# Early zero transfers on GpSimd's queue, and node counts summed by VectorE before TensorE

## The chip, the cores and the metric

The kernel runs on one core of a Trainium2 chip. The metric is the device time of one execution in microseconds. TensorE (PE) multiplies matrices, VectorE (DVE) and ScalarE (ACT) do elementwise work, GpSimd (POOL) does elementwise work and issues transfers, and SyncE (SP) only issues transfers. SP and POOL each have a transfer queue of their own, as ACT has.

## The reference

A two-layer graph network on 625 nodes with 1024 features. What the change touches is in the first layer: an edge list with eight edge types is turned into counts, for every type a table of how many edges run from each node to each node, and the messages are means over them.

```python
def _rgcn(x, edge_index, edge_type, weight, root, bias):
    src, dst = (edge_index[0], edge_index[1])
    msgs = x[src]
    out = x @ root + bias
    n = x.shape[0]
    for r in range(weight.shape[0]):
        mask = (edge_type == r).astype(x.dtype)
        sums = jax.ops.segment_sum(msgs * mask[:, None], dst, num_segments=n)
        cnt = jax.ops.segment_sum(mask, dst, num_segments=n)
        mean = sums / jnp.maximum(cnt, 1.0)[:, None]
        out = out + mean @ weight[r]
    return out
```

A gate, a linear attention and two feed-forward blocks stand around it; the second layer uses the counts of all types again.

## The kernel before

Weights stream from memory in chunks of 128 x 512: SP loads a chunk into one of four staging buffers, an engine splits it into a high part (`w_hi`) and a low part (`w_lo`), and TensorE multiplies with both (`three`, lines 363 to 365). A load waits until the chunk four places ahead of it is split. A group is eight chunks; its results, five tiles of 125 rows, go from PSUM to a ring in SBUF and from there, by POOL's queue, to memory (`pre`). Groups 0 to 9 run first.

**Scatter stage, beside groups 3 to 5.** VectorE works out a position for every edge (ranks, tables, `packed_buckets`, which gives the mark `mk_ranked`). Then 15 scatter steps follow, each with 11 columns of edges. In a step VectorE writes two one-hot tiles for each column (`sc_hi`, `sc_lo`, lines 912 and 913), ScalarE scales one (`sc_code`, line 918), TensorE multiplies them (line 923) between the dense matmuls, and one weight chunk is split: its high part on ScalarE after the third column, its low part on VectorE after the fifth. Step s splits chunk 36 + s. After step 8 VectorE evacuates group 4 (line 479); for that the ring's tiles must have been stored.

The counts are gathered in `adj`, a tile of 125 partitions and 40 x 626 16-bit integers, in the SBUF that the rank tables occupied. It must be zeroed after the tables and before the first counts are added (at 231.9 us). 19 transfers from a tile of zeros do that, each 125 rows by 2636 bytes, on SP's queue: eight in a row after the load of chunk 39, then one after each of the next 11 loads (line 1051). The tile of zeros is written by ScalarE after the evacuation of group 2 (line 1045).

**Relation loop, from about 375 us.** For each of eight edge types VectorE turns the five count tiles (five times 125 source nodes) into a high and a low half-precision part (`a_hi`, `a_lo`). TensorE multiplies ones by them and accumulates all five tiles, which gives the number of edges into each node (`counts_pe`, line 1353: five matmuls for each of two column halves; the low parts are skipped by a branch unless a count is large). VectorE turns that into a reciprocal (`rcnt`). TensorE aggregates node features by counts (line 1406, 160 matmuls a round), VectorE multiplies by the reciprocal (`mtmp`, line 1556), ScalarE copies the high part (line 1456) and VectorE subtracts for the low part (line 1548). Two dense groups follow, with one head pair of an attention between their matmuls (lines 1371 to 1392, VectorE's front of it at lines 1506 to 1513). The counts of the next round are multiplied between the two dense groups.

Each engine runs its own program in order, and the waits between them are on semaphores. These lines give the order on SP:

```python
            if c == LAST_AHEAD:
                wait(SP, mk_zeros)
                wait(SP, mk_ranked)
                for i in range(EARLY):
                    zero_counts(i)
            if c > LAST_AHEAD:
                zero_counts(EARLY + c - LAST_AHEAD - 1)
```

Of the kernel before, what the change touches and what calls it, by code (L numbers as in the profile page):

```python
# [18 lines left out]
P, T = 125, 5  # L19
# [34 lines left out]
def build(nc, a, out):  # L54
# [226 lines left out]
    for g in range(G_PRE0):  # L281
        for m in range(T):
            POOL.wait_ge(S("bank_free"), (g + 1) * T + m + 1)
            if g in TURNED0:
                b, c = PIECES[m]
                POOL.dma_start(pre_t0[L0_ORDER[g] - 4, b][:, c], ring_t[:, b, c]).then_inc(S(f"stpre0_{m}"), 16)
            else:
                POOL.dma_start(pre[L0_ORDER[g], m], ring[:, m, :]).then_inc(S(f"stpre0_{m}"), 16)  # L288

    POOL.wait_ge(S("split_done"), NST + C_BACK)  # L290
    POOL.wait_ge(S("rcnt"), 1)
    for c in range(C_BACK, C_BACK + (-C_BACK) % NSL):
        split_chunk(c, c % NSL, c // NST + 1)
    split_rounds(C_BACK + (-C_BACK) % NSL, C_PROJ + KT)
    POOL.wait_ge(S("feed_full"), KT)
    for g in range(2):
        POOL.dma_start(z[:, :, g * 512:(g + 1) * 512], pre[2 + g].rearrange("t p f -> p t f")).then_inc(S("ld_z"), 16)
    for c in range(C_PROJ + KT, C_L1):
        split_low(c, c % NSL)
    POOL.wait_ge(S("split_done"), NST + C_L1 + NSL)  # L300
    split_rounds(C_L1 + NSL, nloop * NSL)
    for c in range(nloop * NSL, NSTREAM):
        split_chunk(c, c % NSL, c // NST + 1)
# [401 lines left out]
    ZERO, ZERO_RUN = NBUCKET * NB // 2 + 1, 659  # L705
    assert ZERO % ZERO_RUN == 0
# [299 lines left out]
    def beside(dense, evacuate_plain, evacuate, evacuate_half, load_bias):  # L1006
# [38 lines left out]
        mk_zeros = sig(ALE.activation(zeros[:], zero[0:P, :].to_broadcast([P, ZERO_RUN]), ACT.Copy), "act_step")  # L1045

# [6 lines left out]
        EARLY = ZERO // ZERO_RUN - 11  # L1053
        for c in range(SC0 * KT, (SC0 + SC_GROUPS) * KT):
            load_chunk(c, c % NSL, (L0_ORDER[c // KT] - c // KT) * KT)
            if c == LAST_AHEAD:
                wait(SP, mk_zeros)
                wait(SP, mk_ranked)
                for i in range(EARLY):
                    zero_counts(i)  # L1060
            if c > LAST_AHEAD:
                zero_counts(EARLY + c - LAST_AHEAD - 1)
        for g in TURNED0:
            for s in range(KT):
                load_block(g * KT + s, s, L0_ORDER[g] * KT, s)
                if g == TURNED0[0] and s < 3:
                    zero_counts(EARLY + 8 + s)
# [46 lines left out]
        DVE.wait_ge(S("ld_bt"), 16 + 16 * (ZERO // ZERO_RUN))  # L1114
# [49 lines left out]
        ALE.wait_ge(S("ld_bt"), 16 + 16 * (ZERO // ZERO_RUN))  # L1164
# [143 lines left out]

    counts_split(0)
# [35 lines left out]
    def counts_pe(r):  # L1345

        PE.wait_ge(S("a_hi"), r + 1)
        for i in range(2):
            bank, h0, hn = ag_bank(i)
            PE.wait_ge(S("ag_free"), r * 18 + i + 1)  # L1350

            def add(a16, t, first, last):
                return PE.matmul(ps[:, bank, 0:hn], ones16[0:P, :], a16[:, t, h0:h0 + hn], start=first, stop=last)

            for t in range(T - 1):
                add(a_hi, t, t == 0, False)
            with PE.If(many):
                PE.wait_ge(S("a_ready"), r + 1)
                for t in range(T):
                    add(a_lo, t, False, False)  # L1360
            add(a_hi, T - 1, False, True).then_inc(S("ag_full"), 1)

# [33 lines left out]
    def relation_pe(r, more):  # L1396
# [45 lines left out]
    counts_pe(0)  # L1442
# [98 lines left out]
    def relation_dve(r, more):  # L1541
# [9 lines left out]
        for j in range(16):  # L1551
# [6 lines left out]

            DVE.wait_ge(S("ag_free"), 3 + r * 18 + i + 1)
            DVE.sem_inc(S("ag_scaled"), 1)  # L1560
# [7 lines left out]
        if more:  # L1568
            counts_split(r + 1)
            DVE.wait_ge(S("a_ready"), r + 2)  # L1570
# [1043 lines left out]
    def evac_turned(g, b):  # L2614

        if (g, b) == (1, 0):
            DVE.wait_ge(S("ld_bt"), 32 + 16 * (ZERO // ZERO_RUN))
# [474 lines left out]
```

## Time and profile before

| what | value |
|---|---|
| median of 3 runs | 1828.2 us (1827.75 to 1829.06) |
| the profiled execution's own time | 1828.82 us |
| its span in the profile | 1827.3 us |
| TensorE busy | 1738.4 us, 95% of the span |
| VectorE busy | 989.4 us, 54% |
| ScalarE busy | 461.8 us, 25% |
| GpSimd busy | 712.6 us, 39% |
| mean granted TensorE clock | 0.979 of full speed |

The span is the time from the first to the last instruction in the profile; 1.5 us of the time lie around it. Busy time is of instructions that compute; issuing a transfer is not in it. TensorE's matmuls overlap, so a busy TensorE may still have room, and only a stretch in which it waits, or the chain of work that ended last, tells what sets the end.

### The profile page before, as it was taken

The page shows a single profiled execution, that of the slowest core. Times are in us where ns is not written, and L with a number is a line of the kernel's source. Part 1 is how long each engine was busy: PE and PEld are TensorE (multiplying, and loading weights), DVE is VectorE, ACT ScalarE, POOL GpSimd, SP SyncE. Part 2 cuts the span into 40 slices and gives each one's busy share as a digit, 9 for nine tenths or more (in the row PEclk, how much of TensorE's full clock was granted, in tenths as well). Part 3 has the DMA queues.
Part 4 walks back from the last instruction along what each step waited for, and adds up shares of the span by engine and source line. Part 5 has one row for each costly group of instructions (what it writes and reads, how often), then busy time and mean ns, then how long its engine had stood idle before and what let it go on. Part 6 is the DMA issues. An engine that isn't in the chain of part 4 may idle for free.

```text
span 1827.3 us, 27442 instructions
## 1 busy us (share of the span) xinstructions
PE 1738.4 (95%) x9548; PEld 1438.4 (79%) x9548; DVE 989.4 (54%) x2498; ACT 461.8 (25%) x888; POOL 712.6 (39%) x613
## 2 busy tenths in 40 slices
PE   6998999999999999999999999846999999999999
PEld 4775699978777777878787877634999888879987
DVE  6997999972625454452526386877613234352311
ACT  3327788930101011010101154433000000111100
POOL 3100010036363544536453544000785551446862
PEclk9999999999999999999999999858999999999999
DMA  4435333243131212122233532110454350113322
GB/s 132 142 115 163 124 109 94 94 129 94 47 97 38 87 40 80 52 68 69 63 89 122 168 113 86 28 48 7 131 183 142 103 155 25 47 47 126 91 72 67
DMA packets 132122, 168.42 MB, mean 92 GB/s; under 512 B 14383, under 2 KB 75963, under 8 KB 131767
## 3 DMA queue, kind: packets, MB, share of 16 engines
q1 hardware_dynamic: 104213, 128.21, 23.6%
q10 hardware_dynamic: 21730, 22.51, 3.8%
q0 software_dynamic: 6080, 16.40, 2.9%
q8 instruction: 60, 0.98, 0.2%
q14 instruction: 39, 0.32, 0.1%
HBM read 135.51 MB, written 25.30 MB: 88 GB/s over the span
## 4 chain that ended last, share of the span: by engine, by line
PE 81%; DVE 10%; DMA 3%; ACT 2%; DVEq 2%; issue 2%; POOL 1%; SPq 1%; ACTq 0%
PE ps L363 21%; PE ps L364 21%; PE ps L365 21%; PE ps L1406 9%; DMA w_stage<-in_stream 2%; PE ps L1001 1%; DVE w_lo L314 1%; PE ps L1371 1%; PE ps L923 1%; DVE key_start L869 1%; POOL w_lo L272 1%; PE ps L1326 1%; SPq L1051 1%; DMA nat<-in_x 1%; DVE scan L784 1%
## 5 line engine op out<-in xcount | busy, mean ns | idle before, releaser
L363 PE MATMUL ps<-w_hi,xt_hi 128*125 128x512 f32 x1320 | 539.4, 409 | 12.1 <-DVE xt_lo L552 3.5
L252 POOL TENSOR_TENSOR w_hi<-w_stage,zero 128x512 fp32r<-128x512 f32 x258 | 278.1, 1078 | 680.0 <-PE ps L365 650.8
L364 PE MATMUL ps<-w_lo,xt_hi 128*125 128x512 f32 x1320 | 523.6, 397 | 0.0
L365 PE MATMUL ps<-w_hi,xt_lo 128*125 128x512 f32 x1320 | 522.0, 395 | 0.0
L255 POOL TENSOR_TENSOR w_lo<-w_stage,w_hi 128x512 fp32r<-128x512 f32 x258 | 351.2, 1361 | 20.2
L363 PEld LDWEIGHTS ps<-w_hi,xt_hi 128*125 128x125 f32 x1320 | 247.0, 187 | 70.9 <-DVE xt_lo L552 4.3
L365 PEld LDWEIGHTS ps<-w_hi,xt_lo 128*125 128x125 f32 x1320 | 246.4, 187 | 63.3
L364 PEld LDWEIGHTS ps<-w_lo,xt_hi 128*125 128x125 f32 x1320 | 246.6, 187 | 53.4
L363 PE MATMUL ps<-xt_hi,w_hi 128*128 128x314 f32 x736 | 240.9, 327 | 0.8 <-DVE ring L2612 0.7
L365 PE MATMUL ps<-xt_hi,w_lo 128*128 128x314 f32 x736 | 226.0, 307 | 0.0
L364 PE MATMUL ps<-xt_lo,w_hi 128*128 128x314 f32 x736 | 225.8, 307 | 0.0
L363 PEld LDWEIGHTS ps<-xt_hi,w_hi 128*128 128x128 f32 x736 | 138.9, 189 | 1.8 <-POOL w_lo L255 1.1
L364 PEld LDWEIGHTS ps<-xt_lo,w_hi 128*128 128x128 f32 x736 | 139.5, 190 | 0.3
L365 PEld LDWEIGHTS ps<-xt_hi,w_lo 128*128 128x128 f32 x736 | 139.0, 189 | 0.0
L1590 DVE TENSOR_TENSOR nat<-nat,ps 125x512 f32<-125x512 f32 x80 | 53.0, 686 | 121.6 <-PE ps L365 121.3
L1456 ACT ACTIVATE xt_hi<-mtmp 128x313 fp32r<-128x313 f32 (+1 forms) x128 | 59.5, 465 | 196.1 <-DVEq L1560 196.1
L1406 PE MATMUL ps<-a_hi,xn_hi 125*128 125x313 f16 (+1 forms) x640 | 106.4, 297 | 2.0 <-DVE mtmp L1556 1.9
L1406 PE MATMUL ps<-a_hi,xn_lo 125*128 125x313 f16 (+1 forms) x640 | 106.3, 296 | 0.0
L309 ACT ACTIVATE w_hi<-w_stage 128x512 fp32r<-128x512 f32 x116 | 71.8, 628 | 102.7 <-PE ps L365 53.7
L971 ACT ACTIVATE counts<-ps 125x628 int16<-125x628 f32 x120 | 82.0, 691 | 20.9 <-PE ps L1001 19.6
L288 POOL DMA_DIRECT2D pre<-ring x30 | 15.9, 534 | 180.0 <-ACT ring L462 98.0
L1406 PEld LDWEIGHTS ps<-a_hi,xn_hi 125*128 125x128 f16 x640 | 61.4, 97 | 27.5 <-DVE mtmp L1556 3.4
(433 smaller groups left out, 2178.5 us busy)
## 6 DMA issues: line engine op xcount, KB each, us to landing
w_stage<-in_stream SPq DMA_DIRECT2D x374, 256.0 KB, 2.7
pre<-ring POOLq DMA_DIRECT2D x30, 250.0 KB, 5.6
adj<-zeros SPq DMA_DIRECT2D x19, 321.8 KB
a_qt<-pre_t SPq DMA_DIRECT2D x18, 312.5 KB, 3.8
a_qt<-pre_t ACTq DMA_DIRECT2D x14, 312.5 KB
pre_t<-ring_t POOLq DMA_DIRECT2D x12, 312.5 KB, 3.1
pre_t<-ring_t ACTq DMA_DIRECT2D x12, 312.5 KB
a_vx<-pre SPq DMA_DIRECT2D x9, 312.5 KB
```

The lines of the kernel that those rows point to most:

```text
L252: POOL.tensor_tensor(w_hi[:, q, :], w_stage[:, q % NST, :], zero[:].to_broadcast([128, 512]), ALU.add).then_inc(S("hi_done"), 1)
L255: POOL.tensor_tensor(w_lo[:, q, :], w_stage[:, q % NST, :], w_hi[:, q, :].bitcast(F32), ALU.subtract).then_inc(S("split_done"), 1)
L272: POOL.tensor_tensor(w_lo[:, q, :], w_stage[:, q % NST, :], w_hi[:, q, :].bitcast(F32), ALU.subtract).then_inc(S("split_done"), 1)
L309: ALE.activation(w_hi[:, c % NSL, :], w_stage[:, c % NST, :], ACT.Copy).then_inc(S("hi_done"), 1)
L314: DVE.tensor_tensor(w_lo[:, c % NSL, :], w_stage[:, c % NST, :], w_hi[:, c % NSL, :].bitcast(F32), ALU.subtract).then_inc(S("split_done"), 1)
L363: PE.matmul(dst, l_hi, r_hi, start=first, stop=False)
L364: PE.matmul(dst, l_hi, r_lo, start=False, stop=False)
L365: return PE.matmul(dst, l_lo, r_hi, start=False, stop=last)
L971: ALE.activation(counts[g % 4][:], ps[0:P, b:b + 2, 0:SPLIT], ACT.Copy).then_inc(S("hi_main"), 1)
L1406: return PE.matmul(dst, x16[:, t, k * 128:(k + 1) * 128], a16[:, t, h0:h0 + hn], start=first, stop=last)
L1456: ALE.activation(xt_hi[:, j // 2, h0:h0 + hn], mtmp[j % 4][:, 0:hn], ACT.Copy).then_inc(S("mt_hi"), 1)
L1590: DVE.tensor_tensor(u_, u_, ps[0:P, m, :], ALU.add).then_inc(S("bank_free"), 1)
```

## The change

The eight early zero transfers go to POOL's queue, ahead of its stores of group 3, with a semaphore of their own; SP keeps the other eleven. ScalarE writes the tile of zeros before the evacuation of group 0. In rounds 2 to 8 VectorE sums the five count tiles as 16-bit integers, splits the one sum into a high and a low half-precision part, and TensorE multiplies ones by these two, for two column halves: four matmuls for ten and no branch. Round 1 keeps the old form. In the aggregation VectorE no longer waits for its own multiply to signal ScalarE; ScalarE waits for the semaphore of the multiply itself.

```diff
+    def gpsimd_program(mk_zeros, mk_ranked, zero_counts):
+
+        for g in range(G_PRE0):
+            if g == 3:
+                wait(POOL, mk_zeros)
+                wait(POOL, mk_ranked)
+                for i in range(EARLY):
+                    zero_counts(POOL, i, "ld_zero")
+            for m in range(T):
+                POOL.wait_ge(S("bank_free"), (g + 1) * T + m + 1)
...
+        mk_zeros = sig(ALE.activation(zeros[:], zero[0:P, :].to_broadcast([P, ZERO_RUN]), ACT.Copy), "act_step")
         for g in range(3):
             ahead = (g + 2) * KT - (2 if g == 0 else 1)
...
-        mk_zeros = sig(ALE.activation(zeros[:], zero[0:P, :].to_broadcast([P, ZERO_RUN]), ACT.Copy), "act_step")
...
-        def zero_counts(i):
-            SP.dma_start(adj[:].bitcast(F32)[:, i * ZERO_RUN:(i + 1) * ZERO_RUN], zeros[:]).then_inc(S("ld_bt"), 16)
...
+        def zero_counts(eng, i, landed):
+            eng.dma_start(adj[:].bitcast(F32)[:, i * ZERO_RUN:(i + 1) * ZERO_RUN], zeros[:]).then_inc(S(landed), 16)
...
             if c == LAST_AHEAD:
                 wait(SP, mk_zeros)
                 wait(SP, mk_ranked)
-                for i in range(EARLY):
-                    zero_counts(i)
             if c > LAST_AHEAD:
-                zero_counts(EARLY + c - LAST_AHEAD - 1)
+                zero_counts(SP, EARLY + c - LAST_AHEAD - 1, "ld_bt")
...
+    def counts_sum(r):
+
+        t_ = adj[:, bass.ds(r * T * NB, T * NB)].rearrange("p (t x) -> p t x", x=NB)
+        DVE.tensor_tensor(tile_pairs[:], t_[:, 0:2], t_[:, 2:4], ALU.add)
+        DVE.drain()
+        DVE.tensor_tensor(tile_sum[:], tile_pairs[:, 0], tile_pairs[:, 1], ALU.add)
+        DVE.drain()
+        DVE.tensor_tensor(tile_sum[:], tile_sum[:], t_[:, 4], ALU.add)
+        DVE.drain()
+        DVE.tensor_copy(sum_hi[:], tile_sum[:])
+        DVE.drain()
+        DVE.tensor_tensor(sum_lo[:], tile_sum[:], sum_hi[:], ALU.subtract).then_inc(S("a_ready"), 1)
...
+    def sums_pe(r):
+
+        PE.wait_ge(S("a_ready"), 2 * r + 1)
         for i in range(2):
             bank, h0, hn = ag_bank(i)
             PE.wait_ge(S("ag_free"), r * 18 + i + 1)
...
+            dst = ps[:, bank, 0:hn]
+            PE.matmul(dst, ones16[0:P, :], sum_hi[:, h0:h0 + hn], start=True, stop=False)
+            PE.matmul(dst, ones16[0:P, :], sum_lo[:, h0:h0 + hn], start=False, stop=True).then_inc(S("ag_full"), 1)
...
-            counts_pe(r + 1)
+            sums_pe(r + 1)
...
-            ALE.wait_ge(S("ag_scaled"), r * 16 + j + 1)
+            ALE.wait_ge(S("ag_free"), r * 18 + j + 6)
...
-
-            DVE.wait_ge(S("ag_free"), 3 + r * 18 + i + 1)
-            DVE.sem_inc(S("ag_scaled"), 1)
...
             counts_split(r + 1)
-            DVE.wait_ge(S("a_ready"), r + 2)
+            counts_sum(r + 1)
+            DVE.wait_ge(S("a_ready"), 2 * r + 3)
```

The order of instructions at the places that matter. On SP, at the end of the loop over the first loads and after it, before the change:

```order
L198 REGISTER_ALU
L198 COMPARE_AND_BRANCH
L185 DMA w_stage<-in_stream 128x512 [waits split_done] x8
L1051 DMA adj<-zeros 125x659 [waits dve_step,act_step]
L1051 DMA adj<-zeros 125x659 x7
L185 DMA w_stage<-in_stream 128x512 [waits split_done]
L1051 DMA adj<-zeros 125x659
```

And with it:

```order
L198 REGISTER_ALU
L198 COMPARE_AND_BRANCH
L185 DMA w_stage<-in_stream 128x512 [waits split_done] x8
L185 DMA w_stage<-in_stream 128x512 [waits split_done,dve_step,act_step]
L1058 DMA adj<-zeros 125x659
```

The load of chunk 40, which stood behind eight zero transfers, now follows the loads of chunks 32 to 39 directly, and one zero transfer follows it. On POOL, from its first loads to the stores of the groups (`pre`, five a group; `pre_t` are groups in turned layout), before the change:

```order
L212 DMA nat<-in_x 125x1024 [waits ld_x2]
L212 DMA nat<-in_x 125x1024
L272 TENSOR_TENSOR w_lo<-w_stage,w_hi 128x512 [waits hi_done] x8
L288 DMA pre<-ring 125x512 [waits bank_free] x30
L286 DMA pre_t<-ring_t 128x625 [waits bank_free] x3
```

And with it:

```order
L212 DMA nat<-in_x 125x1024 [waits ld_x2]
L212 DMA nat<-in_x 125x1024
L272 TENSOR_TENSOR w_lo<-w_stage,w_hi 128x512 [waits hi_done] x8
L295 DMA pre<-ring 125x512 [waits bank_free] x15
L1058 DMA adj<-zeros 125x659 [waits dve_step,act_step]
L1058 DMA adj<-zeros 125x659 x7
L295 DMA pre<-ring 125x512 [waits bank_free] x15
```

The eight zero transfers stand between the stores of group 2 and those of group 3. On VectorE, in the body of the relation loop after the last low part of the aggregation, before the change:

```order
L1304 COPY a_hi<-adj 125x3130
L1305 REGISTER_ALU
L1306 TENSOR_TENSOR a_lo<-adj,a_hi 125x3130
L1572 ISA
L1572 TENSOR_TENSOR adj<-adj 125x3130
L1506 TENSOR_REDUCE a_mx<-ps 125x8 x2
```

And with it:

```order
L1311 COPY a_hi<-adj 125x3130
L1312 REGISTER_ALU
L1313 TENSOR_TENSOR a_lo<-adj,a_hi 125x3130
L1324 ISA
L1324 TENSOR_TENSOR tile_pairs<-adj 125x1252
L1326 TENSOR_TENSOR tile_sum<-tile_pairs 125x626
L1328 ISA
L1328 TENSOR_TENSOR tile_sum<-tile_sum,adj 125x626
L1330 CAST sum_hi<-tile_sum 125x626
L1332 TENSOR_TENSOR sum_lo<-tile_sum,sum_hi 125x626
L1603 REGISTER_ALU
L1605 ISA
```

Five computing instructions stand between the split of the counts and the addition that carries the counts of all types along (line 1572 before, 1605 now), behind which the attention's front follows.

## Rows read from the trace of the kernel before

**Rows 1.** Page, part 1: busy us, share of the span and instructions of each engine.

```profile
PE 1738.4 (95%) x9548; PEld 1438.4 (79%) x9548; DVE 989.4 (54%) x2498; ACT 461.8 (25%) x888; POOL 712.6 (39%) x613
```

**Rows 2.** Windows: us, busy us of each engine, TensorE clock, DMA share, GB/s.

```profile
160.00:170.00 10.00, 4.97 (x19) 2.78 (x18) 4.12 (x22) 4.00 (x11) 0.00 (x0) 0.76 0.50 168
```

**Rows 3.** Chain that ended last, around 142 us: start us, us, what.

```profile
142.14 23.30 DMA w_stage<-in_stream
```

**Rows 4.** Timeline of SP: start us, us, instruction, count.

```profile
129.80 12.30 SPq L1051 DMA_DIRECT2D adj<-zeros  x8
142.14 2.89 SPq L185 DMA_DIRECT2D w_stage<-in_stream  x1
```

**Rows 5.** Timeline of ScalarE, scatter steps 2 to 4 (brackets: idle before, releaser).

```profile
150.13 0.61 ACT L309 ACTIVATE w_hi<-w_stage 128x512 fp32r<-128x512 f32 x1
...
155.01 0.61 ACT L309 ACTIVATE w_hi<-w_stage 128x512 fp32r<-128x512 f32 x1
...
165.47 0.63 ACT L309 ACTIVATE w_hi<-w_stage 128x512 fp32r<-128x512 f32 x1 [5.49 <-DMA w_stage<-in_stream]
```

**Rows 6.** Timeline of VectorE, scatter steps 0, 4 and 8.

```profile
138.07 0.69 DVE L314 TENSOR_TENSOR w_lo<-w_stage,w_hi 128x512 fp32r<-128x512 f32 x1 [0.28 <-ACT w_hi L309]
...
166.13 0.69 DVE L314 TENSOR_TENSOR w_lo<-w_stage,w_hi 128x512 fp32r<-128x512 f32 x1 [5.88 <-ACT w_hi L309]
...
188.35 3.27 DVE L479 TENSOR_TENSOR ring<-ps,bias_pre 125x512 f32<-125x512 f32 x5
```

**Rows 7.** Timeline of TensorE, scatter steps 4 and 8.

```profile
160.22 0.48 PE L923 MATMUL ps<-sc_hi,sc_code 125*128 125x240 bf16 x3
...
166.44 0.67 PE L923 MATMUL ps<-sc_hi,sc_code 125*128 125x240 bf16 x2 [5.03 <-ACT sc_code L918]
...
186.92 0.48 PE L923 MATMUL ps<-sc_hi,sc_code 125*128 125x240 bf16 x3
```

**Rows 8.** Chain that ended last, relation loop: counts, aggregation of two rounds.

```profile
431.03 1.35 PE ps L1353 x10
...
544.93 21.35 PE ps L1406 x160
...
628.46 21.35 PE ps L1406 x160
```

**Rows 9.** Transfers, 131 to 141 us: GB/s in 40 slices; packets, MB, engines' share.

```profile
GB/s 107 197 229 246 229 188 148 139 130 117 145 116 137 127 127 127 105 127 137 116 137 127 127 137 116 137 127 116 137 127 137 116 127 137 127 127 127 137 116 127
...
q1 hardware_dynamic: 612, 1.39, 36.6%
```

**Rows 10.** Transfers, 16 to 25 us: GpSimd's queue (packets, MB, share); its loads.

```profile
q0 software_dynamic: 288, 1.02, 46.0%
...
nat<-in_x POOLq DMA_DIRECT2D x2, 500.0 KB, 6.2
```

**Rows 11.** Timeline of VectorE, the last table of ranks.

```profile
126.33 0.40 DVE L906 SCALAR_TENSOR_TENSOR g_start<-g_bucket,g_half 1x240 int32<-1x240 f32 x1
```

**Rows 12.** Timeline of GpSimd, 110 to 146 us, and its stores' time to landing.

```profile
113.39 0.53 POOL L288 DMA_DIRECT2D pre<-ring  x1 [0.17 <-issue]
142.11 2.64 POOL L288 DMA_DIRECT2D pre<-ring  x5 [28.18 <-ACT ring L462]
...
DMA to landing us min/median/max: 2.7/5.6/15.0
```

**Rows 13.** Timeline of ScalarE, between groups 0 and 1.

```profile
54.26 1.28 ACT L309 ACTIVATE w_hi<-w_stage 128x512 fp32r<-128x512 f32 x2 [7.00 <-DMA w_stage<-in_stream]
```

**Rows 14.** Timeline of VectorE in one round, before the attention's front.

```profile
570.81 2.38 DVE L1572 TENSOR_TENSOR adj<-adj  x1 [0.17 <-DVE a_lo L1306]
579.02 1.29 DVE L1506 TENSOR_REDUCE a_mx<-ps 125x8 f32<-125x512 f32 x2 [5.83 <-PE ps L1371]
```

**Rows 15.** Instructions on `adj`: ns min/median/max, first and last start, forms.

```profile
L1304 DVE CAST a_hi<-adj x8: 970/972/976, 372.7 to 901.9; 125x3130 f16 x7, 125x3130 f16<-125x3130 int16 x1
...
L1596 DVE TENSOR_REDUCE va<-adj x1: 3408/3408/3408, 985.4 to 985.4; 125x5 f32<-125x3130 int16 x1
```

**Rows 16.** Timeline of the first round's aggregation.

```profile
379.51 2.10 DVE L1500 RECIPROCAL rcnt<-rcnt 128x312 f32<-128x312 f32 x1
...
382.36 0.84 PE L1406 MATMUL ps<-a_hi,xn_hi 125*128 125x313 f16 x5 [1.43 <-DVE mtmp L1556]
```

More of the change, by code:

```diff
@@ L279, in build @@
     PIECES = [(0, slice(0, NODES)), (1, slice(0, NODES)), (2, slice(0, NODES)), (3, slice(0, 314)), (3, slice(314, NODES))]
[L281 to L300, printed above, removed]
@@ L301, in build @@
-    split_rounds(C_L1 + NSL, nloop * NSL)
-    for c in range(nloop * NSL, NSTREAM):
-        split_chunk(c, c % NSL, c // NST + 1)
+    def gpsimd_program(mk_zeros, mk_ranked, zero_counts):
[7 more added lines that the diff above has]
+                POOL.wait_ge(S("bank_free"), (g + 1) * T + m + 1)
+                if g in TURNED0:
+                    b, c = PIECES[m]
+                    POOL.dma_start(pre_t0[L0_ORDER[g] - 4, b][:, c], ring_t[:, b, c]).then_inc(S(f"stpre0_{m}"), 16)
+                else:
+                    POOL.dma_start(pre[L0_ORDER[g], m], ring[:, m, :]).then_inc(S(f"stpre0_{m}"), 16)
+        POOL.wait_ge(S("split_done"), NST + C_BACK)
+        POOL.wait_ge(S("rcnt"), 1)
+        for c in range(C_BACK, C_BACK + (-C_BACK) % NSL):
+            split_chunk(c, c % NSL, c // NST + 1)
+        split_rounds(C_BACK + (-C_BACK) % NSL, C_PROJ + KT)
+        POOL.wait_ge(S("feed_full"), KT)
+        for g in range(2):
+            POOL.dma_start(z[:, :, g * 512:(g + 1) * 512], pre[2 + g].rearrange("t p f -> p t f")).then_inc(S("ld_z"), 16)
+        for c in range(C_PROJ + KT, C_L1):
+            split_low(c, c % NSL)
+        POOL.wait_ge(S("split_done"), NST + C_L1 + NSL)
+        split_rounds(C_L1 + NSL, nloop * NSL)
+        for c in range(nloop * NSL, NSTREAM):
+            split_chunk(c, c % NSL, c // NST + 1)
@@ L705, in build @@
     ZERO, ZERO_RUN = NBUCKET * NB // 2 + 1, 659
+    EARLY = ZERO // ZERO_RUN - 11
     assert ZERO % ZERO_RUN == 0
@@ L1066, in beside @@
                 if g == TURNED0[0] and s < 3:
-                    zero_counts(EARLY + 8 + s)
+                    zero_counts(SP, EARLY + 8 + s, "ld_bt")
         for c in range(C_REL, C_REL + AHEAD):
@@ L1113, in beside @@
             split_dve(chunk_beside(s))
-        DVE.wait_ge(S("ld_bt"), 16 + 16 * (ZERO // ZERO_RUN))
+        DVE.wait_ge(S("ld_bt"), 16 + 16 * (ZERO // ZERO_RUN - EARLY))
+        DVE.wait_ge(S("ld_zero"), 16 * EARLY)
         DVE.wait_ge(S("sc_pe"), sc_per + EC + 1)
@@ L1163, in beside @@
             dense(h + HI0, hist_step(h))
-        ALE.wait_ge(S("ld_bt"), 16 + 16 * (ZERO // ZERO_RUN))
+        ALE.wait_ge(S("ld_bt"), 16 + 16 * (ZERO // ZERO_RUN - EARLY))
+        ALE.wait_ge(S("ld_zero"), 16 * EARLY)
         wait(ALE, mk_slots)
@@ L1307, in counts_split @@
                           ALU.subtract).then_inc(S("a_ready"), 1)
+    tile_pairs = at("tile_pairs", [P, 2, NB], I16, R_EXTRA)
+    tile_sum = at("tile_sum", [P, NB], I16, R_EXTRA + 2560)
+    sum_hi = at("sum_hi", [P, NB], F16, R_EXTRA)
+    sum_lo = at("sum_lo", [P, NB], F16, R_EXTRA + 1280)
+    def counts_sum(r):
[9 more added lines that the diff above has]
+        DVE.tensor_tensor(sum_lo[:], tile_sum[:], sum_hi[:], ALU.subtract).then_inc(S("a_ready"), 1)
     counts_split(0)
@@ L1343, in ag_bank, with counts_pe @@
         return 5 + i % 3, *halves[i % 2]
-    def counts_pe(r):
-        PE.wait_ge(S("a_hi"), r + 1)
+    def counts_pe():
+        PE.wait_ge(S("a_hi"), 1)
         for i in range(2):
             bank, h0, hn = ag_bank(i)
-            PE.wait_ge(S("ag_free"), r * 18 + i + 1)
+            PE.wait_ge(S("ag_free"), i + 1)
             def add(a16, t, first, last):
@@ L1357, in counts_pe @@
             with PE.If(many):
-                PE.wait_ge(S("a_ready"), r + 1)
+                PE.wait_ge(S("a_ready"), 1)
                 for t in range(T):
@@ L1361, in counts_pe @@
             add(a_hi, T - 1, False, True).then_inc(S("ag_full"), 1)
+    def sums_pe(r):
+        PE.wait_ge(S("a_ready"), 2 * r + 1)
+        for i in range(2):
+            bank, h0, hn = ag_bank(i)
+            PE.wait_ge(S("ag_free"), r * 18 + i + 1)
+            dst = ps[:, bank, 0:hn]
+            PE.matmul(dst, ones16[0:P, :], sum_hi[:, h0:h0 + hn], start=True, stop=False)
+            PE.matmul(dst, ones16[0:P, :], sum_lo[:, h0:h0 + hn], start=False, stop=True).then_inc(S("ag_full"), 1)
     def att_pe_b(r):
@@ L2616, in evac_turned @@
         if (g, b) == (1, 0):
-            DVE.wait_ge(S("ld_bt"), 32 + 16 * (ZERO // ZERO_RUN))
+            DVE.wait_ge(S("ld_bt"), 32 + 16 * (ZERO // ZERO_RUN - EARLY))
         if g - 1 not in TURNED1:
```

4 lines of the change are left out of this document (2 added, 2 removed).

## Prediction

> **What bounds the kernel now.** I read the page first, then the stretches in which TensorE waits, then the rows of the two places that the change touches. TensorE is busy 95% of the span [rows 1], so only two kinds of edit can move the end: one that takes away a TensorE stall, and one that takes matmuls out of a stretch where TensorE never waits. The change tries both.
>
> The stall lies in the scatter stage. In 160 to 170 us TensorE is busy 4.97 of 10 us, VectorE 4.12 and ScalarE 4.00, at a mean clock of 0.76 [rows 2]: all three wait together. The chain of waits names the cause, a weight chunk that took 23.30 us from issue to landing [rows 3]. SP's timeline shows why: it issues eight zero transfers in one run of 12.30 us, and only then, at 142.14, chunk 40 [rows 4]. ScalarE splits one chunk in each scatter step, 4.88 us apart (150.13, 155.01); the next split, of chunk 40, comes at 165.47 after 5.49 us of waiting for that load [rows 5]. VectorE, next in line, waits 5.88 us for ScalarE [rows 6], and TensorE 5.03 us [rows 7].
>
> The second place is the loop over relations. One round's 160 aggregation matmuls run as an unbroken piece of the chain, and so do the ten count matmuls between the two dense groups, 1.35 us [rows 8]: TensorE waits for nothing there, so what is cut from it comes off the end.
>
> **Eight zeros go from SP's queue to GpSimd's.** Their price on SP's queue: with zeros almost alone in flight the transfer engines are a third busy and move about 130 GB/s, so 8 x 321.8 KB (2.64 MB) need some 20 us, and chunk 40 stands behind them in the same queue [rows 9]. Loads of the same 125 rows on GpSimd's queue do better: two of them, 1.02 MB, took 46.0% of the time of 16 engines in a window of 9 us, beside SP's own transfers [rows 10], where SP's zeros with the queue almost to themselves get 36.6% [rows 9]. That is 66 us of engine time, so 2.64 MB need 171, or 10.7 us if all 16 share it; by the zeros' own 36.6% of 10 us for 1.39 MB [rows 9] it is 7.0. I expect the eight to land in about 10 us. They can start when the rank tables are done, after VectorE's last row of them at 126.33 + 0.40 [rows 11]. GpSimd is free then: its last store of group 2 is issued at 113.39 and its next, of group 3, only at 142.11; at about 0.7 us from issue to issue the eight take some 6 us [rows 12]. Nothing else waits behind them on GpSimd, and the stores of group 3 find their queue empty even if the zeros ran at SP's 130 GB/s to about 148 and pushed them back by 6 us, since VectorE asks for them only in its evacuation of group 4 (188.35 before, 182.8 after the shift below) [rows 6].
>
> The Trainium skill ("DMA: Bandwidth & Descriptors", section on why a DMA increments its semaphore by 16) says that a hardware queue uses the largest number of engines up to 16 that divides the rows, and GpSimd's queue can use 16 for a direct copy. 125 rows would give 5 of 16, or 31%; the trace's third and its 46.0% agree.
>
> Chunk 40 may be issued when chunk 36 is split, at 138.07 + 0.69 = 138.8 [rows 6], and SP is now free to do it. It has until 159.9 to land, 21 us; the loads between SP's other eleven zeros stay as they are. The 5.49 us wait then goes. The next limit is the step itself: 165.47 - (155.01 + 4.88) = **5.58 us**. VectorE carries this on, as it sets the 4.88 us pace and evacuates group 4. TensorE's own lag was larger: its first scatter matmuls of step 8 come at 186.92, and four steps after those of 160.22 they would come at 179.74, 7.2 us earlier [rows 7]; part of that is the low clock after its stall. VectorE does not gain that surplus, so 7.2 is the upper bound; 4.9 the lower, if a load lands 0.7 us late somewhere.
>
> **The zero tile is written earlier.** One ScalarE instruction moves from about 127.7 to about 41 us. There ScalarE soon waits 7.00 us for a load [rows 13], which hides its 0.7 us. Cost nothing; without that cover 0.7.
>
> **Count matmuls.** Seven of the eight rounds run ten matmuls before and four after: 6/10 of 1.35 = 0.81 us a round, **5.67 us**. The two skipped branches a round go too; I give them nothing. Bounds: 3.2 us, if a gap like the 2.5 us of issue idle over nine times (0.28 each) comes to show at each join and eats as much again (7 x 0.46); 6.5, if the slow first matmul behind them shortens too.
>
> VectorE pays for it with five instructions between the relation's last split and the attention's front. 16-bit adds of 3130 columns take 2.38 us [rows 14], 0.76 ns a column. So the pair sum (1252 columns) is about 1.0 us, two sums of 626 0.55 each, the copy 0.27 (0.972 us for 3130 [rows 15]), the difference 0.45, with drains about 3.2 us. From both sides: 1.6 us if all run as fast as the copy, 4.9 us as slow as the 16-bit reduction (3.408 us for 3130 [rows 15]). Behind them stands the attention's front, which today idles 5.83 us for TensorE's projection [rows 14]. Even 4.9 fits. Without that cover up to 4.9 us a round would fall on ScalarE's exponential, and then on TensorE's transposes.
>
> **The semaphore between multiply and copy goes.** VectorE no longer waits for its own multiply in order to signal ScalarE. In rounds 2 to 8 TensorE waits for neither. In the first round it does: 1.43 us at 382.36, behind a reciprocal that starts at 379.51, 0.15 us after the multiply before it ended [rows 16]. Two such gaps: **0.3 us**; bounds 0 and 1.0.
>
> **Sum.** 5.58 + 5.67 + 0.3 = 11.55 us. The profiled execution took 1828.82, so 1817.3 for it; it lies 0.6 above the median of the runs, so against the median of 1828.2 I say **1816.7 us**, with 1813.5 to 1820.1 from the bounds (8.1 to 14.7).
>
> **Rivals.**
>
> *Half the zeros' gain.* The transfers still run on the same engines, and only SP's time at issuing is saved. Then chunk 40 lands as long after its issue as before, but is issued 3.3 us earlier (138.8 for 142.14): 1828.2 - 3.3 - 5.67 - 0.3 = 1818.9. The third-busy row speaks against it: the delay is order within one queue, not full engines. Chance 0.08. The Trainium skill states this rule in the same page, section "Issuing engines are not separate DMA queues": issuing from several engines saves only the sequencer's time.
>
> *No gain from the zeros*, because another load is late in its place, say one of those after SP's remaining zeros: 1822.2. Those have 18 us and more to land. Chance 0.05.
>
> *No gain from the counts*, if four short matmuls with three waits show as long as ten did: 1822.4. Chance 0.05.
>
> *Slower: GpSimd's queue holds up the stores of group 3.* They stand behind the zeros in its order: 8 x 321.8 + 5 x 250.0 KB, 3.92 MB, must land between 126.7 and 182.8, or VectorE stops in its evacuation, with the scatter columns and splits queued behind it. That takes 70 GB/s; at 55 the stores land at 198, 15.2 us late, and the kernel is 0.2% slower than before. At 50 GB/s it would be 22.3 us: 1839.0. For it speaks a landing of 15.0 us for one of these stores [rows 12], against it that five of them needed only about 17 us then (75 GB/s) beside SP's zeros. Chance 0.04.
>
> *The change does nothing in sum*, both gains given back: 1828, chance 0.04.
>
> **How the numbers follow.** The forecast has 0.74. 0.2% (3.7 us) is about what a measurement can tell from no change. Faster by more: 0.74 + 0.08 + 0.05 + 0.05 = 0.92; same 0.04; slower 0.04. The range of 8 in 10 takes in the first rival and the forecast's bounds: 1813 to 1821.
>
> **What would show it.** ScalarE's splits of chunks 36 to 43 stand 4.9 us apart with no wait for a load but one at most, and the 0.76 clock is gone. Chunk 40 lands under 10 us after its issue. GpSimd's zero transfers keep the engines well above a third. A round of the relation loop falls from 83.5 (544.93 to 628.46 [rows 8]) to 82.7 us. VectorE's idle before the attention's front falls to about 2.6 us. I am wrong if a load or a store takes the wait over in 140 to 200, or if TensorE shows gaps around the four matmuls.

## The result and the profile after

The changed kernel takes 1817.44 us (median of 4 runs, 1816.58 to 1818.49) where the one before took 1828.63 beside it (4 runs, 1827.75 to 1829.64): ratio 0.9942, 95% interval 0.9926 to 0.9957, 11.2 us faster. The forecast was 1816.7 in a range of 1813 to 1821. The profiled execution took 1818.19 us, its span 1816.8 where that of before was 1827.3.

The page's first part [rows 1]: TensorE lost 42 matmuls (seven rounds, six fewer in each) and 6.5 us of busy time; VectorE gained 34 us of it, which no term of the sum had.

```profile
PE 1731.9 (95%) x9506; PEld 1434.6 (79%) x9506; DVE 1023.1 (56%) x2533; ACT 461.8 (25%) x888; POOL 717.8 (40%) x621
```

**The scatter stage.** The windows of the changed kernel, columns as in [rows 2]:

```profile
130.00:140.00 10.00, 10.00 (x48) 7.57 (x47) 9.46 (x24) 2.27 (x7) 2.31 (x5) 1.00 1.00 261
...
160.00:170.00 10.00, 10.00 (x57) 6.34 (x55) 9.44 (x49) 8.94 (x26) 0.00 (x0) 1.00 0.41 134
```

TensorE's hole in 160 to 170 is gone, with it the 0.76 of its clock. In 130 to 140 the transfer engines are busy all the time and move 261 GB/s, where for most of 131 to 141 they moved about 130 before [rows 9]. The list of transfers from 126 to 143 us says by which queue, and how long a transfer took to land:

```profile
q0 software_dynamic: 591, 2.46, 59.0%
q1 hardware_dynamic: 585, 1.07, 24.1%
...
adj<-zeros POOLq DMA_DIRECT2D x8, 321.8 KB, 9.6
```

GpSimd's queue alone has 59.0% of the engines' time, and a zero transfer lands 9.6 us after its issue. The view of the line that issues them adds the last start and the longest landing:

```profile
L1058 POOL DMA_DIRECT2D adj<-zeros x8: 530/530/533, 128.1 to 131.8; - x8
...
DMA to landing us min/median/max: 4.0/9.6/13.3
```

So the last of the eight has landed by 145.1 (131.8 + 13.3). SP's timeline, in place of the run of eight zeros [rows 4], and ScalarE's splits of chunks 39 to 41 [rows 5]:

```profile
128.35 11.62 SPq L185 DMA_DIRECT2D w_stage<-in_stream  x5
140.02 0.85 SPq L1058 DMA_DIRECT2D adj<-zeros  x1
```

```profile
155.79 0.61 ACT L316 ACTIVATE w_hi<-w_stage 128x512 fp32r<-128x512 f32 x1
160.67 0.61 ACT L316 ACTIVATE w_hi<-w_stage 128x512 fp32r<-128x512 f32 x1
165.54 0.62 ACT L316 ACTIVATE w_hi<-w_stage 128x512 fp32r<-128x512 f32 x1
```

Chunk 40 is the last of the five loads, issued by 139.97 and landed 6.1 us after its issue. Its split follows that of chunk 39 after 4.88 us and without a wait, where it took 10.46 before: 5.58 us less, to the hundredth.

Two waits of TensorE's are left between 140 and 215 us. One, of 1.94 us at 145.62, stood there before too (1.80 at 144.83). The other comes at VectorE's evacuation of group 4 and has grown, from 0.65 us before to 1.92; behind it the granted clock of 190 to 200 falls to a mean of 0.85, between its two levels of 1.2 and 2.4 GHz, where it was 1.00 before. The evacuation itself starts without a wait; its line stands first here, then TensorE's:

```profile
183.55 3.08 DVE L486 TENSOR_TENSOR ring<-ps,bias_pre 125x512 f32<-125x512 f32 x5
...
187.47 0.99 PE L931 MATMUL ps<-sc_hi,sc_code 125*128 125x240 bf16 x3 [1.92 <-ACT sc_code L926]
```

**The relation loop.** The chain of the changed kernel, at the count matmuls of the first round and at the aggregation of the two rounds that stand in [rows 8]:

```profile
425.43 0.15 PE ps L1395
425.58 0.13 PE ps L1396
425.71 0.13 PE ps L1395
425.84 0.13 PE ps L1396
...
537.73 21.35 PE ps L1441 x160
...
620.46 21.35 PE ps L1441 x160
```

Four matmuls run in 0.54 us with no gap where ten took 1.35, and a round takes 82.73 us instead of 83.53. The sums cost VectorE more than forecast. Its timeline in the round of [rows 14], and GpSimd's in the same microseconds:

```profile
563.25 1.65 DVE L1324 TENSOR_TENSOR tile_pairs<-adj 125x1252 int16 x1
564.98 1.42 DVE L1326 TENSOR_TENSOR tile_sum<-tile_pairs 125x626 int16<-125x626 int16 x1
566.57 1.07 DVE L1328 TENSOR_TENSOR tile_sum<-tile_sum,adj 125x626 int16<-125x626 int16 x1 [0.17 <-issue]
567.72 1.26 DVE L1330 CAST sum_hi<-tile_sum 125x626 f16<-125x626 int16 x1
569.05 0.49 DVE L1332 TENSOR_TENSOR sum_lo<-tile_sum,sum_hi 125x626 f16<-125x626 int16 x1
569.70 2.66 DVE L1605 TENSOR_TENSOR adj<-adj  x1 [0.16 <-DVE sum_lo L1332]
572.28 1.27 DVE L1541 TENSOR_REDUCE a_mx<-ps 125x8 f32<-125x512 f32 x2
```

```profile
562.66 1.57 POOL L252 TENSOR_TENSOR w_hi<-w_stage,zero 128x512 fp32r<-128x512 f32 x1 [22.46 <-PE ps L372]
564.31 1.75 POOL L255 TENSOR_TENSOR w_lo<-w_stage,w_hi 128x512 fp32r<-128x512 f32 x1
566.20 1.09 POOL L252 TENSOR_TENSOR w_hi<-w_stage,zero 128x512 fp32r<-128x512 f32 x1
567.38 1.42 POOL L255 TENSOR_TENSOR w_lo<-w_stage,w_hi 128x512 fp32r<-128x512 f32 x1
```

The five take 6.3 us (563.25 to 569.54), not 3.2, and VectorE no longer idles before the attention's front (L1541). Measured from the start of the round's aggregation the front comes 0.46 us later than before (34.55 us against 34.09). TensorE waits for none of it.

### The profile page after: what moved, and what is told of

Its sections match the earlier page's. It is cut to its first block, busy times and chain, and to the rows that moved or that the text cites. A ratio compares the mean times of both kernels' runs of the same rounds, so it can differ in the third digit from the quotient of the medians.

```text
span 1816.8 us, 27294 instructions
## 1 busy us (share of the span) xinstructions
PE 1731.9 (95%) x9506; PEld 1434.6 (79%) x9506; DVE 1023.1 (56%) x2533; ACT 461.8 (25%) x888; POOL 717.8 (40%) x621
## 4 chain that ended last, share of the span: by engine, by line
PE 80%; DVE 11%; ACT 3%; DMA 2%; DVEq 2%; issue 2%; POOL 0%; ACTq 0%; SPq 0%
PE ps L370 21%; PE ps L371 21%; PE ps L372 21%; PE ps L1441 9%; PE ps L1009 2%; ACT sc_code L926 1%; DVE w_lo L321 1%; DMA z<-pre 1%; PE ps L1406 1%; DVE key_start L877 1%; PE ps L1351 1%; DMA nat<-in_x 1%; DVE scan L792 1%; PE ps L1416 0%; PE ps L2509 0%
## 5 line engine op out<-in xcount | busy, mean ns | idle before, releaser
L1591 DVE TENSOR_TENSOR mtmp<-ps,rcnt 128x313 f32<-128x313 f32 (+1 forms) x128 | 61.7, 482 | 45.4 <-PE ps L1441 44.3
```

The lines of the kernel that those rows point to most:

```text
L1591: DVE.tensor_tensor(mtmp[j % 4][:, 0:hn], ps[:, bank, 0:hn], rcnt[:, h0:h0 + hn], ALU.mult).then_inc(S("ag_free"), 1)
```

## Experiments

All runs stand in one table: the time, its ratio to the kernel before measured beside it, and three marks of each trace. Stretch A runs from ScalarE's split of chunk 39 to the first relation's cast of its counts (`a_hi`), B from there to the last relation's cast, C from there to the end of the span. Six of the seven changed count blocks lie in B, the seventh in C. The kernel before took 1828.63 us beside the changed kernel, 1829.24 beside zeros_only, counts_only, semaphore_back and zeros_spread, 1829.63 beside zeros_act, sums_twice, sums_alone and two_matmuls, and 1829.26 beside the last two.

| kernel | median us | ratio, interval | chunk 39 | first cast | last cast | span | A | B | C |
|---|---|---|---|---|---|---|---|---|---|
| before | 1828.63 | | 155.01 | 372.72 | 901.95 | 1827.3 | 217.71 | 529.23 | 925.4 |
| changed | 1817.44 | 0.9942, 0.9926-0.9957 | 155.79 | 368.17 | 891.44 | 1816.8 | 212.38 | 523.27 | 925.4 |
| zeros_only | 1823.18 | 0.9966, 0.9954-0.9978 | 155.58 | 367.77 | 896.93 | 1820.2 | 212.19 | 529.16 | 923.3 |
| counts_only | 1822.39 | 0.9961, 0.9947-0.9975 | 156.09 | 373.86 | 897.22 | 1821.6 | 217.77 | 523.36 | 924.4 |
| semaphore_back | 1817.23 | 0.9943, 0.9930-0.9957 | 156.81 | 368.69 | 892.97 | 1815.2 | 211.88 | 524.28 | 922.2 |
| zeros_spread | 1820.34 | 0.9959, 0.9946-0.9973 | 155.10 | 369.95 | 893.24 | 1816.2 | 214.85 | 523.29 | 923.0 |
| zeros_act | 1819.15 | 0.9948, 0.9935-0.9962 | 154.75 | 368.79 | 892.03 | 1817.1 | 214.04 | 523.24 | 925.1 |
| sums_twice | 1817.64 | 0.9934, 0.9920-0.9948 | 155.17 | 367.55 | 890.84 | 1816.3 | 212.38 | 523.29 | 925.5 |
| sums_alone | 1820.65 (one run) | | 155.33 | 367.54 | 894.16 | 1819.3 | 212.21 | 526.62 | 925.1 |
| two_matmuls | 1815.53 | 0.9924, 0.9910-0.9937 | 156.23 | 368.59 | 890.16 | 1814.4 | 212.36 | 521.57 | 924.2 |
| low_part_branch | 1814.57 | 0.9923, 0.9909-0.9936 | 154.86 | 367.19 | 888.81 | 1813.1 | 212.33 | 521.62 | 924.3 |
| changed_again | 1817.95 | 0.9934, 0.9920-0.9948 | 154.88 | 367.25 | 890.55 | 1816.6 | 212.37 | 523.30 | 926.1 |

The intervals are 0.12 to 0.16% wide to either side, 2.2 to 2.8 us: they tell each part from the kernel before, but not one part from the other, nor single microseconds. A and B repeat far better: B is 523.24 to 523.36 us in the six traces with the changed kernel's relation loop (sums_twice, which changes only VectorE's part of it, among them).

### Each part alone

zeros_only is the kernel before with the zeros' part of the diff, counts_only the one with the rest:

```diff
# zeros_only
+                for i in range(EARLY):
+                    zero_counts(POOL, i, "ld_z")
# counts_only
-            counts_pe(r + 1)
+            sums_pe(r + 1)
...
-            ALE.wait_ge(S("ag_scaled"), r * 16 + j + 1)
+            ALE.wait_ge(S("ag_free"), r * 18 + j + 6)
```

> Only the eight zero transfers move to GpSimd's queue; count matmuls and the semaphore stay as before (the zeros count on a semaphore that is free until later). My theory (chunk 40 no longer stands behind the zeros, the step pace of 4.88 us is the next limit): the split of chunk 40 comes 4.88 us after that of chunk 39, the end of the scatter stage moves by 5.58 us, the kernel is 5.6 us faster (ratio 0.9969), 5.0 at the least if the wait at the evacuation of group 4 grows. Rival, that the zeros gave only SP's issue time: 3.3 us (0.9982). Rival, that what the trace of the whole change shows at 370 us (4.5 us) is all that is left of it at the end: 4.5 us (0.9975).

> Only the count matmuls and the semaphore change; the zeros stay on SP's queue and the 5.49 us wait for chunk 40 stays. My theory after the trace of the whole change: 7 x 0.80 us of matmuls and 1.06 us in the first round, 6.7 us faster (ratio 0.9963); the period of a round is 82.7 us. By the terms of the prediction (0.3 us for the semaphore): 6.0 us (0.9967). Rival, that the join costs as much as the matmuls saved: about 1 us or less. If the two parts add up, this and the kernel with the zeros alone give 11 to 12 us together.

Measured: 6.1 us (1829.24 - 1823.18) and 6.9 us (1829.24 - 1822.39). In the traces zeros_only shortens A by 5.52 us and leaves B (0.07), counts_only shortens B by 5.87 and leaves A (0.06). By the stretches the parts add up (5.52 + 5.87 against 5.33 + 5.96 in the changed kernel), and each has its own place. By the medians they give 13.0 us against 11.2, which the intervals allow but which shows no sum. The rivals with half the zeros' gain or none, and with none from the counts, fall: 3.3 us, and also 4.5, lie below A's 5.5.

### The semaphore put back

```diff
-            ALE.wait_ge(S("ag_free"), r * 18 + j + 6)
+            ALE.wait_ge(S("ag_scaled"), r * 16 + j + 1)
...
+            DVE.wait_ge(S("ag_free"), 3 + r * 18 + i + 1)
+            DVE.sem_inc(S("ag_scaled"), 1)
```

The zeros are counted on the semaphore `ld_z` here, as in zeros_only; the rest is the changed kernel.

> The changed kernel with the semaphore between multiply and copy put back: VectorE waits for its own multiply and then signals ScalarE, as before. If the 1.06 us that the first round gained beyond the matmuls is the semaphore's: TensorE's waits for the mean at the start of the first round come back (about 1.4, 0.45 and 0.5 us in place of less), the aggregation of round 2 starts 1.0 us later, measured from the end of the histogram stage, and the rounds from the second on keep 82.7 us; the kernel is 1 us slower than the changed one, about 10 us faster than before (ratio 0.9944). If it is 0.3 us as predicted: round 2 starts 0.3 us later. Rival, that the later rounds also hang on it: their period grows beyond 82.8 us.

Against the changed kernel's 523.27, B is 1.01 us longer. From the first cast to the aggregation of round 2 it is 0.91 of that, and the later rounds keep 82.73 us, so the rival with a longer period falls. TensorE's waits from 360 to 400 us, of this kernel and of the changed one (in total, times, longest):

```profile
PE ps L1441 <- DVE mtmp L1591: 1.9, 2, 1.4
```

```profile
PE ps L1441 <- DVE mtmp L1591: 1.2, 1, 1.2
```

0.7 us of the 1.0 are these waits, all in the first round. VectorE runs behind TensorE there (in the changed kernel until 388 us, here past 391), so each multiply's wait for itself (0.23 us between `mtmp` and the next instruction) adds up over many multiplies, not over two. The total time, 1817.23, is not the 1 us above the changed kernel that was expected: its C is 3.1 us shorter, in stages of which the edit touches only the last round's multiplies.

### Order in the queue, or engines to carry it

Two other ways to take the eight zeros out from in front of chunk 40, both on a hardware queue: behind the loads on SP's own queue, and on ScalarE's.

```diff
# zeros_spread: on SP, behind each load from chunk 40 on
                 zero_counts(SP, EARLY + c - LAST_AHEAD - 1, "ld_bt")
+                zero_counts(SP, c - LAST_AHEAD - 1, "ld_zero")
# zeros_act: on ScalarE, behind each of its first eight splits
+                    if s < EARLY:
+                        if s == 0:
+                            wait(ALE, mk_ranked)
+                        zero_counts(ALE, s, "ld_zero")
```

> The changed kernel, but the eight zeros go back to SP's queue, one more behind each of the eight loads from chunk 40 on, so that chunk 40 itself stands in front of them. If the gain came from the order in one queue alone, and the rate in it is enough: 4.88 us from split to split, the same time as the changed kernel (0 to 0.5 us from it). If the rate of one hardware queue with 125 rows limits it (two zeros of 321.8 KB at 130 GB/s need 4.95 us, a load more, in a step of 4.88): each load lands later than the one before, by 1 to 2 us a step, and the wait for a load comes back after some six steps, with 3 to 10 us; the kernel is then 3 to 10 us slower than the changed one.

> The changed kernel, but the eight zeros are issued by ScalarE on its own queue, one behind each of its splits from 130 us on, in place of GpSimd's queue. If a queue of its own is what counts: 4.88 us from split to split to the end of the stage and the time of the changed kernel (within 1 us). If the few transfer engines that a hardware queue uses for 125 rows count, as with the zeros spread over SP's queue: SP's own zeros and ScalarE's need the same engines, loads land later and later, and a wait of 2 to 3 us comes back at the end of the stage, near 200 us, as it did there. If ScalarE is held up while it issues (SP's issues took 1.5 us each when its queue was full): steps of more than 4.88 us, up to 8 us in sum.

In both the split of chunk 40 follows after 4.9 us, without a wait; in zeros_spread

```profile
155.10 0.62 ACT L313 ACTIVATE w_hi<-w_stage 128x512 fp32r<-128x512 f32 x1
159.98 0.62 ACT L313 ACTIVATE w_hi<-w_stage 128x512 fp32r<-128x512 f32 x1
```

and in zeros_act from 154.75 to 159.62. The order was the cause of the stall of before. But a smaller wait comes back later. In zeros_spread ScalarE's splits near 200 us read

```profile
197.81 0.63 ACT L313 ACTIVATE w_hi<-w_stage 128x512 fp32r<-128x512 f32 x1 [0.62 <-DMA w_stage<-in_stream]
...
204.96 0.63 ACT L313 ACTIVATE w_hi<-w_stage 128x512 fp32r<-128x512 f32 x1 [2.16 <-DMA w_stage<-in_stream]
```

and in zeros_act

```profile
198.84 0.63 ACT L313 ACTIVATE w_hi<-w_stage 128x512 fp32r<-128x512 f32 x1 [2.04 <-DMA w_stage<-in_stream]
```

A is 2.47 and 1.66 us longer than in the changed kernel. From 126 to 215 us the loads' median time from issue to landing says why; the rows are of the changed kernel, zeros_spread and zeros_act:

```profile
w_stage<-in_stream SPq DMA_DIRECT2D x19, 256.0 KB, 4.3
```

```profile
w_stage<-in_stream SPq DMA_DIRECT2D x18, 256.0 KB, 11.7
```

```profile
w_stage<-in_stream SPq DMA_DIRECT2D x19, 256.0 KB, 10.1
```

A hardware queue of its own (ScalarE's) helps little: the loads land almost as late as with all zeros on SP's. Getting out of the order gives 5.58 us at chunk 40. What GpSimd's queue adds is that the eight are through by 145.1 us, ahead of most of the loads; with this A is 1.7 to 2.5 us shorter than in the two others, where a wait comes back near 200. These two runs change the time of issue with the queue: ScalarE issues its eight one a step, from 137.16 to 174.01, and GpSimd all of them from 128.1 to 131.8. So they don't show whether the early issue or the wider queue is worth the 1.7 to 2.5 us; no run issues the eight early, in one block, on a hardware queue other than SP's. The expectation by rate had the right kind and place, though for SP's queue a larger price (3 to 10 us). ScalarE was not held up: its first issue takes 1.35 us and the others 0.72 to 0.76, and they hide in its idle time. In total zeros_spread lies 2.9 us above the changed kernel's 1817.44 and zeros_act 1.7, differences that the intervals don't part.

### What VectorE's sums cost, and how much is hidden

```diff
# sums_twice
+            counts_sum(r + 1, False)
             counts_sum(r + 1)
# sums_alone: once, where GpSimd splits nothing
     counts_split(0)
+    counts_sum(1, False)
```

> The changed kernel with the five sum instructions once more, without a signal, right after the split of the first relation's counts at 371 us, where GpSimd does nothing; what they compute there is thrown away. If VectorE's sums are slow in the rounds because GpSimd's splits run beside them: here the pair sum takes about 0.95 us, the two sums of 626 columns 0.5 each, the cast 0.2 to 0.3, the difference 0.49, about 2.7 us in all with their gaps. If these instructions are as slow by themselves: 1.65, 1.42, 1.07, 1.26 and 0.49 us as in the rounds, 6.3 us in all. The time of the kernel rises by what the five take, since the first round waits for VectorE.

> The changed kernel with VectorE's five sum instructions done twice in each of the seven rounds; the results are the same. In the changed kernel the exponential ends at 576.99 and TensorE's transposes behind it come at 582.06, so about 5.1 us of cover are left a round. My theory (the five cost 6.3 us as they stand, beside GpSimd's splits): the attention's front comes about 6.3 us later, 1.2 us beyond the cover, TensorE waits some 1 to 1.5 us before the transposes in each round and the kernel is 7 to 11 us slower than the changed one (ratio to before 0.998 to 1.000). By the prediction's price (3.2 us), or if the second pass is faster because GpSimd has no more to split: all inside the cover, no difference (0.994).

In sums_alone the five instructions read

```profile
370.25 0.81 DVE L1324 TENSOR_TENSOR tile_pairs<-adj 125x1252 int16<-125x1252 int16 x1
371.48 0.49 DVE L1326 TENSOR_TENSOR tile_sum<-tile_pairs 125x626 int16<-125x626 int16 x1 [0.43 <-issue]
372.04 0.49 DVE L1328 TENSOR_TENSOR tile_sum<-tile_sum,adj 125x626 int16<-125x626 int16 x1
372.60 0.33 DVE L1330 CAST sum_hi<-tile_sum 125x626 f16<-125x626 int16 x1
373.00 0.49 DVE L1332 TENSOR_TENSOR sum_lo<-tile_sum,sum_hi 125x626 f16<-125x626 int16 x1
```

That is 3.24 us, the price of the prediction; B is 3.35 us longer for it. The other 3.1 us are paid for company: in the rounds each of the slow four ends 0.2 to 0.7 us after the GpSimd instruction beside it (GpSimd ends at 564.23, 566.06, 567.29 and 568.80, VectorE at 564.90, 566.40, 567.64 and 568.98), and the fifth, with GpSimd idle, takes its 0.49. GpSimd's own splits grow in turn, from 1.04 and 1.29 us to 1.57 and 1.75. The Trainium skill ("SBUF — State Buffer", section "SBUF: two separate sides") says that GpSimd and VectorE share a pair of ports by an exclusive lock, VectorE when it is in a two-port fast mode, or when it has two SBUF inputs and the GpSimd instruction reads SBUF; the one that starts first has it for the whole instruction. These ends agree.

My expectation of sums_twice failed: I expected 7 to 11 us, and there is nothing (1817.64; B 523.29). In the same round of sums_twice the second pass, the add and the front read

```profile
569.01 0.81 DVE L1324 TENSOR_TENSOR tile_pairs<-adj 125x1252 int16 x1
569.89 1.17 DVE L1326 TENSOR_TENSOR tile_sum<-tile_pairs 125x626 int16<-125x626 int16 x1
571.13 1.42 DVE L1328 TENSOR_TENSOR tile_sum<-tile_sum,adj 125x626 int16<-125x626 int16 x1
572.63 0.33 DVE L1330 CAST sum_hi<-tile_sum 125x626 f16<-125x626 int16 x1
573.03 0.48 DVE L1332 TENSOR_TENSOR sum_lo<-tile_sum,sum_hi 125x626 f16<-125x626 int16 x1
573.68 1.79 DVE L1610 TENSOR_TENSOR adj<-adj  x1 [0.16 <-DVE sum_lo L1332]
575.38 1.28 DVE L1545 TENSOR_REDUCE a_mx<-ps 125x8 f32<-125x512 f32 x2
```

The second pass costs 4.5 us, and the add behind it only 1.79 in place of 2.66. Against the times without company (1.79 us for the add) VectorE loses 4.9 us in this round, with seven of GpSimd's split instructions beside its sums and add. In the changed kernel it loses 4.15 in the same round, with six, and 3.3 in the first round, with four. That is 0.7 to 0.8 us for each of them, so in these rounds the loss goes by their number and not by the amount of VectorE's work. So the front comes about 3.7 us later (575.38 against 572.28, in a trace that is 0.6 us early), and the exponential ends at 580.09 (578.72 + 1.37), 1.4 us ahead of TensorE's transposes (ScalarE's row, then TensorE's):

```profile
578.72 1.37 ACT L1498 ACTIVATE a_qkf<-a_qkf,a_eps 125x1280 f32<-125x1280 f32 x1 [19.23 <-DVE a_qkf L1552]
...
581.45 0.70 PE L1418 MATMUL ps<-ident,a_qkf 125*128 125x125 f32 x5
```

The cover is thus 5.1 us in the changed kernel (576.99 to 582.06), and no more than 1.4 of it is left here. No run went beyond it.

### Fewer matmuls still

```diff
# two_matmuls
-            PE.matmul(dst, ones16[0:P, :], sum_hi[:, h0:h0 + hn], start=True, stop=False)
-            PE.matmul(dst, ones16[0:P, :], sum_lo[:, h0:h0 + hn], start=False, stop=True).then_inc(S("ag_full"), 1)
+            PE.matmul(dst, ones16[0:P, :], sum_hi[:, h0:h0 + hn], start=True, stop=True).then_inc(S("ag_full"), 1)
# low_part_branch: the same where no bucket holds over 409 edges
-        DVE.tensor_scalar(flag_i[:], flag[:], 2048.0, None, ALU.is_gt)
+        DVE.tensor_scalar(flag_i[:], flag[:], 409.0, None, ALU.is_gt)
...
+            with PE.If(many):
...
+            with PE.Else():
+                PE.matmul(dst, ones16[0:P, :], sum_hi[:, h0:h0 + hn], start=True, stop=True).then_inc(S("ag_full"), 1)
```

> The changed kernel with two count matmuls in place of four in seven rounds: the low part of the sums is left out (it is zero as long as a sum is at most 2048). If a matmul of 313 columns without a wait costs its share of the chain (0.13 us): 14 x 0.13 = 1.9 us faster than the changed kernel, 82.46 us a round; ratio to before 0.993. If the pair costs a fixed time at its start (the first matmul behind a wait): less than 1 us.

> The changed kernel with the two matmuls of the low part behind a branch that is taken only where a bucket of edges holds more than 409 of them (five times 409 is under 2048, so below that the low part of a sum is zero); the flag of the kernel gets that lower threshold, and nothing is left out. With the branch not taken two count matmuls run in a round. If the branch costs TensorE as little as the two skipped branches between the ten matmuls of before: 0.28 us a round as in the kernel with two matmuls, 1.7 to 1.9 us faster than the changed kernel, about 1815.5 us, a round of 82.45. If a branch ahead of the matmuls shows, because TensorE has nothing queued behind it: a gap of some 0.3 us at each of two branches a round, 7 x 0.6 = 4.2 us, and the kernel is 2.4 us slower than the changed one.

> The changed kernel once more, beside the one with the branch, as the base of that comparison and to see how far two traces of one kernel lie apart by themselves. If the stages behind the relation loop vary by themselves: the stretch from the last relation's split of the counts to the end, 925.4 us in the first trace of the changed kernel, comes out anywhere from 922 to 926 as in the other kernels. If the change itself shifts these stages: 925.4 again within 0.5 us. All of the time: 1817 to 1818 us, a round of 82.73.

two_matmuls shortens B by 1.70 us, six rounds of 0.28, low_part_branch by 1.68 against changed_again: the branch not taken costs nothing that B shows. Two rounds and their counts, from the chain of low_part_branch:

```profile
536.22 21.35 PE ps L1444 x160
589.36 0.29 PE ps L1399 x2
618.66 21.35 PE ps L1444 x160
```

The round is 82.44 us, where the changed kernel has 82.73. low_part_branch has the lowest median of all, 1814.57 beside 1817.95 for the changed kernel measured with it; their intervals overlap (0.9909 to 0.9936, 0.9920 to 0.9948), and of the 3.4 us between them B and the seventh round explain 2.0.

## Why the prediction was right

**The stall was order within SP's queue: right, to size.** 5.58 us was forecast from 165.47 - (155.01 + 4.88); the split of chunk 40 moved by that, and at the end of stretch A 5.33 (changed), 5.34 (changed_again) and 5.52 us (zeros_only) of it are left. Where the last 0.1 to 0.25 us go was not followed; the wait behind the evacuation of group 4, 1.3 us longer than before, is one candidate. The rival of half the gain gave 3.3 us. The rule that stood beside it (the Trainium skill, "DMA: Bandwidth & Descriptors", section "Issuing engines are not separate DMA queues") counts only the sequencer's time; here the measurement decides otherwise, since waiting behind a neighbour in one queue is not in that rule, and zeros_spread shows it without any second issuer.

**GpSimd's queue would use more of the engines: right.** Forecast were about 10 us to land and well above a third of the engines; the rows show 9.6 us and 59.0%. On hardware queues, issued later, the zeros get in the loads' way to the end of the stage.

**GpSimd's stores of group 3 would not be late: right.** VectorE's evacuation of group 4 starts at 183.55 with no wait; 182.8 was forecast, in a trace that ran 0.8 us late at chunk 39 already.

**The zero tile: right, as far as it shows.** Its 0.75 us on ScalarE come at 41.60, and the wait for a load behind them is 6.83 us. The 0.78 us by which chunk 39 is late are not its price: changed_again writes the tile at the same place and splits chunk 39 at 154.88, counts_only writes it where the kernel before does and splits it at 156.09.

**Four count matmuls for ten: right.** 0.81 us a round were forecast and are measured (0.54 for 1.35; a period shorter by 0.80). No gap came up at the joins. (The rival without a gain from the counts should read 1822.3, not 1822.4; nothing hangs on it.)

**The semaphore: right in kind, the term too small.** "Two such gaps: 0.3 us" should have been 1.0, at its upper bound. The prediction counted the gaps behind the two reciprocals. The self-wait recurs at each multiply for as long as VectorE is behind, and the wait of 0.45 us after the one of 1.43 goes with it.

**VectorE's five instructions: the price failed, the conclusion held.** "From both sides: 1.6 to 4.9 us" missed 6.3, because the rows it was scaled from were taken as the instruction's own cost. The row for the 16-bit add, 2.38 us for 3130 columns [rows 14], already had GpSimd's splits in it: the same add takes 1.79 at 404.35 in the changed kernel's first round, where GpSimd is idle, and in sums_twice. That the price so scaled, 3.2 us, meets the 3.24 of sums_alone is chance. The idle expected before the front, 2.6 us, is zero. The 5.83 us of idle time, the cover that the prediction counted on, were used up. Nothing came of it, since the way on, which the prediction had named but not measured (the exponential, then the transposes), held 5.1 us more, and sums_twice used 3.7 of it for nothing. So this conclusion held by a cover that the prediction had not counted, which is luck.

**The sum.** By the traces: A 5.33, B 5.96 and the seventh count block 0.81 make 12.1 us; the spans differ by 10.5 and the medians by 11.2. Of the 1.6 us between 12.1 and 10.5, 0.8 went ahead of chunk 39, which this trace splits 0.78 us later than that of before, and 0.8 in C, which should be shorter by the seventh block and is not. C is 922.2 to 926.1 us over the twelve traces, and 925.4 and 926.1 in two of the same kernel; of the diff only that block, the last round's sums and its multiplies run there. What makes C vary was not found. The total, 11.2 us where 11.55 was forecast, is close partly by luck: the zeros were 0.2 too large and the semaphore 0.7 too small, and 0.9 us of the 12.1 does not show in the medians.

## What to carry to other kernels

When a load is late, look first at what stands ahead of it in its own queue: a new order removed the stall in each of the three ways tried. Then look at when the other transfers get through, and how many transfer engines their queue can use for such a shape: only the eight issued early on GpSimd's queue kept a smaller stall from coming back. On a kernel whose TensorE is 95% busy, matmuls cut from a stretch without waits came off the round to the hundredth of a microsecond (0.81 forecast, 0.80 measured), so work is worth handing to an engine with slack, and then worth cutting again (0.28 us a round behind a branch). Price VectorE work from rows in which GpSimd does the same as it will at the new place, and look for the second cover before counting the overflow of the first.

## What was not expected of the hardware

Beside GpSimd's splits VectorE's short instructions take two to four times as long: 0.33 us alone and 1.26 in company for a cast of 626 columns, 0.49 and 1.42 for an add. The loss went by the number of GpSimd's instructions in the stretch: twice the sums cost VectorE 3.7 us more there, not 6.3.

Transfers from 125 rows on ScalarE's own hardware queue delayed SP's loads almost as much (10.1 us to land) as on SP's queue (11.7), while the same bytes on GpSimd's, issued earlier and in one block, left them at 4.3.
